# Three attentions of a decoder: one VectorE instruction for mask, scale and maximum, reciprocals two items at a time, one more turned copy on VectorE

## The reference

```python
# L1x, cross attention of layer 1 (16 heads of 16), mask of queries x keys
score = jnp.where(mask == 0, -1e20, q @ k.T)
out = softmax(score / 4) @ v
# L2x, cross attention of layer 2 (one head of 256)
weights = softmax(q @ k.T / 16 + mask * -1e9)
# L3x, latent attention of layer 3 (8 heads of 64), keys = 256 context + 256 own tokens
sim = jnp.where(full_mask, q @ k.T / 64, -3.4e38)
out = softmax(sim) @ v
# L1a, attention of layer 1 (16 heads of 16), causal, scores weighted by distance
attn = softmax(where(causal, -inf, relu(q @ k.T) * R_hat) / 4)
```

## Time and profile before

| what | value |
|---|---|
| median of 3 runs | 3799.43 us (3787.58 to 3802.03) |
| profiled execution, first to last instruction | 3782.3 us |
| L1a, its loop | about 1582 to 1811 |
| L1x, its loop | about 1844 to 2108 |
| L2x | about 2622 to 2670 |
| L3x, its loop | about 3136 to 3502 |
| busy over the whole span | PE 79%, DVE 62%, ACT 47%, POOL 19% |

### The profile page before, as it was taken

One profiled execution on the slowest core, in us unless ns is written; L12 is line 12 of the kernel. 1 busy time (PEld: TensorE's weight loads), 2 busy tenths in 40 slices (PEclk: granted clock), 3 DMA queues, 4 the chain that ended last, 5 costly groups with the idle time before them and its releaser, 6 DMA issues. The chain is left out here.

```text
span 3782.3 us, 54983 instructions
## 1 busy us (share of the span) xinstructions
PE 2988.6 (79%) x18517; PEld 2137.4 (57%) x18517; DVE 2358.6 (62%) x5264; ACT 1790.9 (47%) x4260; POOL 719.5 (19%) x833
## 2 busy tenths in 40 slices
PE   6889988998877888377677671596799858888697
PEld 5667766676656567255455331444598435555485
DVE  6776777667566423777678768697511485555423
ACT  6666666666432222577577364402333325556221
POOL 2000000000110322155345100000111002334422
PEclk8999999999989799699899885798799979999798
DMA  3110111011100477000000000000497101000476
GB/s 122 37 34 29 46 37 37 26 48 32 42 4 1 146 248 260 16 2 2 25 10 4 26 0 0 3 0 10 150 349 266 48 25 36 24 24 12 151 256 212
DMA packets 109525, 264.75 MB, mean 70 GB/s; under 512 B 16928, under 2 KB 71456, under 8 KB 104384
## 3 DMA queue, kind: packets, MB, share of 16 engines
q1 hardware_dynamic: 92896, 228.95, 18.1%
q0 software_dynamic: 8688, 23.78, 1.7%
q10 hardware_dynamic: 7664, 8.51, 0.7%
HBM read 213.65 MB, written 47.54 MB: 69 GB/s over the span
## 5 line engine op out<-in xcount | busy, mean ns | idle before, releaser
L3019 POOL TENSOR_TENSOR L0a_sum_sq<-L0a_sum_sq,L0a_sq 128x512 f32<-128x512 f32 x56 | 76.5, 1366 | 890.6 <-ACT L0a_sq L2942 890.6
L1296 POOL TENSOR_TENSOR L3x_p<-L3x_p,L3x_rsum 128x512 f32<-128x512 f32 x128 | 133.0, 1040 | 445.1 <-DVE L3x_rsum L1377 445.1
L3093 DVE SCALAR_TENSOR_TENSOR L0a_xf<-L0a_xc,L0a_conv,L0a_xf 128x256 f32<-128x256 f32 x432 | 191.3, 510 | 21.7 <-ACT L0a_xf L2907 20.4
L2847 ACT ACTIVATE L0a_ex<-bank,L0a_nb 128x128 f32<-128x128 f32 x512 | 144.7, 368 | 96.8 <-PE bank L2776 96.2
L3102 DVE TENSOR_TENSOR L0a_ru<-bank,L0a_um 128x512 f32<-128x512 f32 x128 | 88.0, 687 | 155.4 <-PE bank L2768 150.2
L1358 DVE SCALAR_TENSOR_TENSOR L3x_s<-bank,L3x_bias 128x512 f32<-128x512 f32 x128 | 86.3, 680 | 131.0 <-PE bank L1136 131.0
L1986 PE MATMUL bank<-L2a_half,L2a_diag 128*128 128x512 f32 x328 | 144.1, 601 | 28.4 <-ACT L2a_diag L1969 28.4
L2692 PE MATMUL bank<-x_feat,L0a_wx 128*128 128x256 f32 x576 | 152.4, 414 | 8.2 <-DVE L0a_coef L3178 6.7
L1296 POOL TENSOR_TENSOR L1x_p<-L1x_p,L1x_rsum 128x512 f32<-128x512 f32 x128 | 132.2, 1040 | 135.7 <-DVE L1x_rsum L1377 135.7
L1300 POOL TENSOR_TENSOR L1a_p<-L1a_p,L1a_rsum 128x128 f32<-128x128 f32 (+1 forms) x256 | 123.0, 506 | 135.9 <-DVE L1a_rsum L1377 133.8
L2692 PEld LDWEIGHTS bank<-x_feat,L0a_wx 128*128 128x128 f32 x576 | 113.5, 205 | 36.7 <-DVE L0a_coef L3178 9.2
(11 more groups left out here) (738 smaller groups left out, 8243.5 us busy)
## 6 DMA issues: line engine op xcount, KB each, us to landing
L2f_wt<-in_L2f_w SPq DMA_DIRECT2D x23, 2180.0 KB, 9.5
L0f_wt<-in_L0f_w SPq DMA_DIRECT2D x39, 898.0 KB, 6.1
L3f_wt<-in_L3f_w SPq DMA_DIRECT2D x39, 768.0 KB, 5.4
L0a_wx<-in_L0a_wx SPq DMA_DIRECT2D x72, 256.0 KB, 3.1
L0a_wz<-in_L0a_wz SPq DMA_DIRECT2D x32, 512.0 KB, 4.3
context_keys_values<-L2f_zeros ACTq DMA_DIRECT2D x32, 256.0 KB, 4.7
L0f_xs<-rows_by_expert SPq DMA_DIRECT2D x39, 128.5 KB, 3.3
L3f_xs<-rows_by_expert SPq DMA_DIRECT2D x39, 128.5 KB, 2.7
```

The costliest lines, as they stand in the source:

```text
L1296: last = nc.gpsimd.tensor_tensor(both, both, rsum[r % 2][:, i, :].unsqueeze(2).to_broadcast([P, S, NK]), ALU.mult)
L2847: last = a(ex[g % 3][:, j, b * P:(b + 1) * P], bank[:, at:at + P], ACT.Exp, bias=nb[r % 2][:, b, h:h + 1])
L3093: vec.scalar_tensor_tensor(out=xf[q % 4][:, j, :], in0=xc[q % 3][:, j, i:i + T], scalar=conv[:, 2 * p + j, i:i + 1], in1=xf[q % 4][:, j, : ...
```

## The change

In L1x, L2x and L3x the two VectorE instructions `scale_mask` and `maximum` become one `tensor_tensor_reduce`: out = (scores + bias) * (-scale), and its minimum is minus the maximum. So `s` holds the negated scores, and the exponential gets scale -1. The instruction has one accumulator, so L1x needs two of them for an item. Reciprocals are made for two items at once, after the second, in L1a, L1x and L3x, and GpSimd waits for the pair. In L1x VectorE copies two of four turned items instead of one. L1a keeps its two instructions.

```diff
-    by_dve = lambda key: twins == 2 and key[0] == "p" and key[1] % G == G - 1
+    by_dve = lambda key: twins == 2 and key[0] == "p" and key[1] % G in ((G - 1,) if causal else (1, G - 1))
...
-                        act.wait_ge(sig("max"), g + 1)
+                        act.wait_ge(sig("max") if causal else s_ring.emptied, g + 1)
...
-                                                 bias=nmax[r % 2][:, i, e:e + 1],
+                                                 bias=nmax[r % 2][:, i, e:e + 1], scale=1.0 if causal else -1.0,
...
-                            pool.wait_ge(sig("reciprocal"), g + 1)
+                            pool.wait_ge(sig("reciprocal"), g // 2 + 1)
...
-                            ins = vec.scalar_tensor_tensor(out=s[:], in0=bank[:, 0:W], scalar=scale,
-                                                           in1=bias[r % 2][:].rearrange("p t s -> p (t s)"), op0=ALU.mult, op1=ALU.add)
+                            for e, (t, at, nk) in enumerate(items[i][1]):
+                                ins = vec.tensor_tensor_reduce(out=s[:, at:at + nk], in0=bank[:, at:at + nk], in1=bias[r % 2][:, e, :],
+                                                               scale=-scale, scalar=3e38, op0=ALU.add, op1=ALU.min,
+                                                               accum_out=nmax[r % 2][:, i, e:e + 1])
...
                         dve.wait_ge(sig("exp"), S * (g + 1))
-                        rs = rsum[r % 2][:, i, :]
+                        rs = rsum[r % 2][:, i - 1:i + 1, :]
                         vec.reciprocal(rs, rs).then_inc(sig("reciprocal"), 1)
...
+                            if d == 2 and not causal and LA <= u < steps + LA:
+                                take_turned((u - LA) * G + 1)
...
-                        if RLAG <= g < total + RLAG:
+                        if RLAG <= g < total + RLAG and (g - RLAG) % 2 == 1:
                             reciprocal(g - RLAG)
...
-                        if g < total:
+                        if causal and g < total:
                             maximum(g)
```

More of the change, by code:

```diff
@@ L1319, in hide @@
                         if kind == "pairs":
-                            vec.tensor_scalar(b_[:], m_[:], 0.0, -1e20 * scale, ALU.is_equal, ALU.mult).then_inc(sig("bias"), 1)
+                            vec.tensor_scalar(b_[:], m_[:], 0.0, -1e20, ALU.is_equal, ALU.mult).then_inc(sig("bias"), 1)
                             dve.wait_ge(sig("bias"), r + 1)
@@ L1365, in maximum @@
                         s, nm = s_sb[g % NSB], nmax[r % 2]
[L1366 to L1370, removed]
+                        for e, (t, at, nk) in enumerate(items[i][1]):
+                            last = vec.tensor_reduce(nm[:, i, e:e + 1], s[:, at:at + nk], AX.X, ALU.max, negate=True)
                         last.then_inc(sig("max"), 1)
@@ L1540, in _ @@
                         if i < n:
-                            act.wait_ge(sig("max"), i + 1)
-                            nc.scalar.activation(prob[i % 3][:], scores[i % 3][:], ACT.Exp, bias=nmax[:, i:i + 1],
+                            act.wait_ge(s_ring.emptied, i + 1)
+                            nc.scalar.activation(prob[i % 3][:], scores[i % 3][:], ACT.Exp, bias=nmax[:, i:i + 1], scale=-1.0,
                                                  accum_out=rsum[:, i:i + 1]).then_inc(sig("exp"), 1)
@@ L1572, in _ @@
                             dve.wait_ge(sig(f"mask{r % 2}"), 16 * (r // 2 + 1))
-                            vec.tensor_scalar(bias[r % 2][:], mask[r % 2][:], -1e9, None, ALU.mult).then_inc(sig("bias"), 1)
+                            vec.tensor_scalar(bias[r % 2][:], mask[r % 2][:], -16e9, None, ALU.mult).then_inc(sig("bias"), 1)
                             dve.wait_ge(sig("bias"), r + 1)
@@ L1577, in _ @@
                             dve.wait_ge(sig("exp"), i - 2)
[L1578 to L1581, removed]
+                        s_ring.empty(vec.tensor_tensor_reduce(out=scores[i % 3][:], in0=bank[:, 0:T], in1=bias[r % 2][:], scale=-1.0 / 16.0,
+                                                              scalar=3e38, op0=ALU.add, op1=ALU.min, accum_out=nmax[:, i:i + 1]))
                         if i >= 3:
```

## The result

| | before | after |
|---|---|---|
| median of 4 runs each | 3794.59 us (3787.58 to 3802.03) | 3875.93 us (3872.70 to 3878.17) |
| profiled execution, first to last instruction | 3782.3 us | 3876.4 us |

The change makes the kernel slower: the ratio of the times is 1.0225, with a 95% interval of 1.02 to 1.0249. The mean granted clock of the profiled execution is 0.897 (1.00 is TensorE at 2.4 GHz, 0.50 at 1.2 GHz).

A forecast was written before the change was run, and what follows sets the result against it. The prediction took TensorE as close to the bound in L3x and a loop of VectorE and TensorE waits in L1x. Its terms, 91 + 12 + 4 - 2 - 3 = +102 on 3799.4, gave about 3900 us, range 3845 to 3970.

The forecast's parts named there:

- The order in L3x: L3x: scores, VectorE's pair reciprocal, GpSimd's division, then turning at 3.26 and weighing at 3.81; an ordinary step 1.25 us longer.
- The step with the output projection at 0: L3x: turning ahead of this projection starts 1.66 us later, which fits in TensorE's earlier idle 1.89, so no cost.
- The clock's term, +12: L3x: TensorE's clock falls behind the `output` step's gap of about 4.9 us, losing 1.7 us in each of seven rows.
- The sign that TensorE's busy time would stay the same: L3x: TensorE's busy time unchanged at 320 us, with the stretch about 465 us long.
- L3x as a whole: L3x: +91 us from waits, with +12 us for TensorE's clock counted separately.
- The fused instruction's price in L1x, +4: L1x: three items at 0.86 us ahead of VectorE's copy, 2.58 for 2.46, in 32 steps; bounds -15 and +30 us.
- The second copy at nothing: L1x: 32 copies of 0.59 us moved from ScalarE to VectorE cost nothing; without cover, 19 us in all.
- L1a -2 and L2x -3: L1a: one reciprocal of 0.07 us less ahead of its copy in 32 steps. L2x: a maximum saved, bounds -6 and +2.
- The rival of half rate: Fused instruction streams at half rate, each 256 columns costing 0.27 us more in L1x, L3x and L2x: 3985 us; 8 in 100.
- The rival of a hidden division: L3x: GpSimd's division stays hidden and the relief counts; with ScalarE setting L1x's step, -21, 3778 us, faster; 7 in 100.
- The rival of the clock in ordinary steps: L3x: the clock also falls in ordinary steps, 1.7 us lost in 20 to 40 of them: 3935 to 3970; 10 in 100.
- The rival of a half-absorbed wait: L3x: slack in already late steps absorbs half the new wait, L3x +50, total 3850 us; 10 in 100.

## Why the prediction was right, and where it was off

The forecast was 3900 with a range of 3845 to 3970; 3875.93 came. The reason given, a new chain through VectorE and GpSimd inside L3x's step, is what the traces show and what two runs isolate. The pairs alone make +109.3 in L3x, and the same pairs one item earlier make none of it. That the number came so near is in part luck. The waits in L3x were well sized. But the clock's term there was half of what came and L1x had the wrong sign, and the two errors cancel in good part: the stages sum to +97 for +102. The base was some 20 us too high, so that 3875.93 lies just inside the narrower range of 3875 to 3930, at its end.

- **The order in L3x**: right. The ordinary steps' turning starts at 3.20 (3.30 in the one shown) and their weighing at 3.76 (3.85); 3.26 and 3.81 were worked out from the earlier trace rows. In the `spread` step the turning starts 4.35 after the scores (3255.20 - 3250.85), 4.40 was implied; in the `output` step 6.49, 6.54 was worked out. Ordinary steps grow by 1.20 to 1.30, predicted 1.25. The step behind `output` grows by 0.84 only, since it had been late before.
- **The step with the output projection at 0**: right. At the full clock it takes 8.69 before and after. The turning's wait takes the place of the idle 1.89 of the earlier trace rows, and the projection then waits 0.22. It runs at the lower clock in two of six rows instead of three, which is the -0.27 of the table.
- **The clock's term, +12**: right in kind, too small. One loss of 1.7 in each row was counted, for the `output` step. Without any clock loss, by the prediction's own waits, `spread` would take 5.49 + 2.39 = 7.88 and `output` 6.19 + 3.85 = 10.04. Two of the six rows do have 7.84 and 7.85 in `spread`, at the full clock; no row has the second value. The means are 9.31 and 12.33, so the clock costs 1.5 and an estimated 2.3 a row, an estimated 23 us over the stage once the last row and the one slow output projection less are counted. The step that was missed is `spread`: behind its gap of 2.64 the clock is down in four of six rows, behind the 4.78 of `output` in all six. The sign that TensorE's busy time would stay the same failed with it: between the first and the last turning it went from 308.2 to 336.5. That is more than the clock alone, since the eight matmuls in one go of 1.09 us became two groups of 0.66 and 0.63.
- **L3x as a whole**: predicted 91 + 12 = 103, measured 109.7, which is about 87 of waits and 23 of clock (an estimate from the step table).
- **The fused instruction's price in L1x, +4**: the wrong sign, -12.9. The term that failed is 0.10 for each read-out, taken "since each must wait for the end of its stream". It is hidden. An item takes 0.69, not 0.86, near the lower bound of 0.66. Three items are 2.07, and 2.07 - 2.46 = -0.39, in 32 steps -12. TensorE's wait for the copy did go from 37.1 to 26.0 us in all. But the output projection waits 2.7 more for ScalarE's `cT` (6.1 for 3.4), and TensorE's idle time in the stage falls by 7.8 only; the other 5.2 of the 12.9 are less busy time at a higher granted clock. So -12 and -12.9 agree by luck, and the gain that the loop explains is 8. The stream's 0.33 was right (0.345 from one start to the next). The formula of the Trainium skill weighed there ("VectorE: DVE Perf Modes", the section on the TRN2 errata) gives 392 ns for 256 columns: further from these 345, and near the 417 that one instruction lasts.
- **The second copy at nothing**: right in this kernel (231.6 and 231.5). In the kernel before L1x was 6.2 longer with it, of which 1.7 are waits; the rest is the clock, which the prediction did not have for L1x and which varies by 3 us there with no change at all.
- **L1a -2 and L2x -3**: +0.4 and +0.2. In L1a TensorE's wait for VectorE's copy did shrink by the 2 us, from 29.9 to 27.7, but its busy time grew by 1.6 at a granted clock of 0.95 for 0.96. In L2x no gain came, and no experiment went after it.
- **Relief in L3x**: not in the prediction as a term. It is -6.6 where the new wait is absent (344.2 to 344.5 for 351.0), mostly from the `output` step and the next, 0.37 each: the two in which VectorE was late. The prediction said that the saved maximum "is in no wait here", which holds for ordinary steps only.
- **The rival of half rate**: refuted, 417 ns for 256 columns and 682 for 512. **The rival of a hidden division**: it is the kernel with the pairs early. The change would have been that, with an RLAG of 2. **The rival of the clock in ordinary steps**: refuted, the ordinary steps keep a granted clock of 1.00 with a gap of 1.48. **The rival of a half-absorbed wait**: refuted by L3x's +109.7.

The terms sum to +97 rather than +102. Most of the rest of the 24 us lies in the base. The prediction started from a median of 3799.43, which is 3794.59 with a fourth run. It took the 17 us between that median and the profiled span for a fixed time around the first and last instruction. That time is only 1.8 us in every execution that has both on record (3878.17 for a span of 3876.4). The rest is spread between executions: the profiled one of before was a quick one, 10 below its median (3782.3 + 1.8 = 3784.1), and that of after lies 2 above its own. So the spans differ by 94 and the medians by 81.

## What to carry to other kernels

- If an operation is made for two items at once, the first of them becomes as late as the second. Count, in the engine's own order, which scores or loads stand ahead of the pair and how long after them the first item is needed. Here one item's place decided between +2.25% and -0.85%.
- When a wait is inserted into a loop of a nearly full TensorE, read the lengths of the matmuls behind the gap, too: about a fifth of this loss was the lower clock (some 23 of 110 us), and it went when the long gaps went.
- When a stage's length agrees with a sum, look at idle and busy time apart. L1x came out at -12.9 for a worked-out -12, and only 7.8 of it were waits; the rest was the clock.
- What a relieved engine gains shows only where it was late. Look for those steps (here `output` and the next) before counting the relief as nothing or as all.

## What the runs showed of the hardware

A pair's division keeps GpSimd busy for 2.04 us on end. A VectorE instruction that starts beside a division and reads one fp32 or int32 tile in SBUF lasts longer. Before, the copy `L1x_cb` took 0.41 to 0.43 and started when the division was over or within its last 0.02 us. The mask's `L1x_bias` took 0.90 beside the single division in seven rows and 0.43 in the one without. After:

```profile
1964.97 2.04 POOL L1296 TENSOR_TENSOR L1x_p<-L1x_p,L1x_rsum 128x512 f32<-128x512 f32 x2 [3.71 <-DVE L1x_rsum L1378]
...
1966.23 1.06 DVE L1311 COPY L1x_cb<-ctx_feat 128x512 f32<-128x512 f32 x1
...
1972.46 2.04 POOL L1296 TENSOR_TENSOR L1x_p<-L1x_p,L1x_rsum 128x512 f32<-128x512 f32 x2 [2.96 <-DVE L1x_rsum L1378]
...
1973.72 1.06 DVE L1320 TENSOR_SCALAR L1x_bias<-L1x_mask 128x512 f32<-128x512 int32 x1
...
3231.66 1.09 POOL L1296 TENSOR_TENSOR L3x_p<-L3x_p,L3x_rsum 128x512 f32<-128x512 f32 x1
...
3231.88 1.01 DVE L1325 TENSOR_SCALAR L3x_bias<-L3x_bias 128x256 f32<-128x256 f32 x1
```

The copy ends at 1967.29 and the division at 1967.01; the other pair ends at 1974.78 and 1974.50. Both end 0.28 after GpSimd is done, as if they began to stream only then; so does `L1x_bias` before (1991.47 for 1991.18). The Trainium skill has this ("SBUF — State Buffer", SBUF: two separate sides): VectorE and GpSimd share a pair of ports, VectorE in its instructions of a 2-port mode, and the one that comes second is blocked until the other's instruction ends. These rows agree with it. Instructions that read a bank in PSUM keep their length beside the same divisions (0.42 at 1970.23 is as long with GpSimd idle as 0.42 at 1972.61 is beside it). The last row, the shift of L3x's mask, isolates it. In the kernel after it takes 1.01 in the six rows of the batch in which it starts beside a division and 0.29 in the two without one. With the pairs early and with single reciprocals no division runs beside it, and it takes 0.29 in all eight. In L1x the longer copy costs nothing: the one at 1966.23 is followed by 2.16 us in which VectorE waits for scores.
